# Merging edge keys in groups of four chunks, with a regular order of gathers and adds and no limit registers, in a four-layer graph kernel

## What is computed

```python
h = jnp.maximum(_layernorm(x, axis=-1), 0.0)
agg = jax.ops.segment_sum(edge_attr_32, src, num_segments=3125)
x = x + mlp_with_batchnorm(jnp.concatenate([h, agg], axis=1))
h = jnp.maximum(_layernorm(x, axis=-1), 0.0)
msg = tensor_product(radial(edge_weight), harmonics(edge_attr_3), h[src])
x = x + zeros.at[dst].add(msg)
h = jnp.maximum(_layernorm(x, axis=-1), 0.0)
x = x + three_rounds(h, weighted_adjacency)
h = jnp.maximum(_layernorm(x, axis=-1), 0.0)
x = x + three_rounds_with_batchnorm(h, counted_adjacency)
```

## Time and profile before

| | us |
|---|---|
| median of three runs | 3673.9 |
| the profiled execution | 3668.75 |
| its span in the profile | 3667.0 |
| PE, DVE, ACT, POOL busy | 3008.7, 2849.6, 2416.7, 2168.8 |
| adds on POOL (784), gathers on POOL (784) | 1298.4, 825.8 |

### The profile page before, as it was taken

The page is one execution under the profiler, slowest core; times in us unless marked ns, Lnnn a source line. Parts: engine busy times, 40 slices in busy tenths (PEclk is TensorE's granted clock), DMA queues, the critical chain, the costliest instruction groups (busy, mean ns, idle before and its releaser), DMA issues. The chain is left out here.

```text
span 3667.0 us, 72915 instructions
## 1 busy us (share of the span) xinstructions
PE 3008.7 (82%) x19605; PEld 2412.6 (66%) x19605; DVE 2849.6 (78%) x7391; ACT 2416.7 (66%) x3535; POOL 2168.8 (59%) x1633
## 2 busy tenths in 40 slices
PE   5777688888779999999999999999999946656656
PEld 4667677777667787788788778777777721113246
DVE  6678999998789899899899899899899844341054
ACT  5789799999677777777777777777777712221000
POOL 4037777777468888888888888888888840000000
PEclk9999899999889999999999999999999968788878
DMA  9964333333232333323223223333323239998840
GB/s 391 421 209 62 33 45 46 46 45 44 25 63 47 48 45 48 47 45 48 47 45 49 45 46 48 46 46 47 48 46 47 45 80 427 425 420 352 362 175 5
DMA packets 293446, 422.80 MB, mean 115 GB/s; under 512 B 153015, under 2 KB 228408, under 8 KB 286856
## 3 DMA queue, kind: packets, MB, share of 16 engines
q0 software_dynamic: 149536, 124.64, 20.3%
q1 hardware_dynamic: 127432, 224.50, 18.5%
q10 hardware_dynamic: 16416, 72.92, 4.9%
HBM read 290.44 MB, written 131.45 MB: 115 GB/s over the span
## 5 line engine op out<-in xcount | busy, mean ns | idle before, releaser
L553 POOL DMA_INDIRECT both<-kept x784 | 1298.4, 1656 | 551.8 <-issue 205.4
L881 PEld LDWEIGHTS ps<-prod,big 128*128 128x128 f32 x7840 | 1194.5, 198 | 199.5 <-DVE prod L1211 189.2
L881 PE MATMUL ps<-prod,big 128*128 128x170 f32 x7840 | 1235.9, 319 | 88.8 <-DVE prod L1211 88.8
L562 POOL DMA_INDIRECT kept<-feat_dram,kept x784 | 825.8, 1053 | 288.2 <-issue 204.9
L872 PE MATMUL ps<-prod,onehot 128*128 128x320 f32 x3920 | 693.2, 324 | 155.9 <-DVE prod L1242 155.7
L640 ACT ACTIVATE big<-iota_b,kept 128x640 f32<-128x640 f32 x1078 | 813.0, 814 | 0.0
L872 PEld LDWEIGHTS ps<-prod,onehot 128*128 128x128 f32 x3920 | 594.5, 193 | 171.9 <-DVE prod L1242 164.4
L645 ACT ACTIVATE big<-big 128x2560 f32<-128x2560 f32 x196 | 458.1, 2337 | 360.8 <-PE ps L881 360.7
L938 PE MATMUL ps<-w2mix,kept 65*128 65x384 f32 x1568 | 585.4, 516 | 42.5 <-ACT kept L688 21.7
L1378 DVE TENSOR_REDUCE kept<-kept 128x80 f32<-128x1280 f32 x392 | 562.2, 1475 | 0.0
L938 PEld LDWEIGHTS ps<-w2mix,kept 65*128 65x128 f32 x1568 | 287.8, 195 | 216.1 <-issue 48.4
(11 more groups left out here) (222 smaller groups left out, 3183.0 us busy)
## 6 DMA issues: line engine op xcount, KB each, us to landing
both<-big POOLq DMA_DIRECT2D x40, 2000.0 KB, 99.3
big<-both SPq DMA_DIRECT2D x50, 1600.0 KB, 11.0
kept<-keys_dram SPq DMA_DIRECT2D x392, 128.0 KB
adj_w<-kept ACTq DMA_DIRECT2D x32, 800.0 KB, 32.3
big<-adj_w SPq DMA_DIRECT2D x32, 800.0 KB, 12.4
big<-adj_w ACTq DMA_DIRECT2D x32, 800.0 KB, 11.5
kept<-in_wT SPq DMA_DIRECT2D x196, 128.0 KB
adj_c<-kept ACTq DMA_DIRECT2D x42, 400.0 KB, 31.9
```

Source lines behind the costliest of these rows:

```text
L553: pool.indirect_dma_start(both, bass.IndirectOffsetOnAxis(ap=sc_idx[:, c:c + 1], axis=0), sc_val[:, c // 2, c % 2, :], None, bounds_check= ...
L562: pool.indirect_dma_start(gath[:, s % 2, k, :], None, feat_dram, bass.IndirectOffsetOnAxis(ap=src_i[:, 4 * s + k:4 * s + k + 1], axis=0), ...
L881: mm = pe.matmul(part_sums(part, MSG), onehot[:, q, k, part * P:(part + 1) * P], prod[:, q, k, 0:HI * MSG], start=False, stop=False, skip_ ...
```

## The change

- In the first stage keys are merged in groups of four chunks, one group for two steps: six squares and one 1536-wide rectifier on ACT for a group (`compare_group`), one 512-wide mask (`mark_group`), one set of entries (`group_entries`). The count of live entries passes from chunk to chunk through `merge_open` and three `merge_hop`.
- Keys come in loads of four chunks, edge attributes in loads of 16 chunks (four steps). The high one-hot factor is made once ahead of the stage. `by_act` gives ACT five of 16 one-hots in four steps where it had six; DVE makes eleven where it made ten.
- POOL issues 392 adds ahead of the feature wait instead of 320; then in every second-stage step four gathers and two adds, two steps behind the gathers (`BEHIND`).
- The adds and gathers no longer name a register with the largest allowed index.

```diff
-FIRST = 320
-TAIL = 16
+GROUPS0 = STEPS // 2
 LOADS_AT, SETUP_AT = 13, 16
-BEHIND = 3
+BEHIND = 2
 WSTAGE, CSTAGE = 6, 6
 TO_PROD = 2 * (RING + KEPT - 4)
...
-        near = edge(2, STEPS)
-        keyrow = edge(2, 2 * P)
-        key_gap = edge(6 * P)
-        same = edge(2, 6, P, dt=BF16)
-        same_tri = edge(2, 2, P, dt=BF16)
-        live = edge(2, 2, dt=BF16)
-        high0 = edge(2, 4, HI)
-        offs = sb("offs", [P, 2])
-        attr = sb("attr", [P, 2, 4, FEAT])
+        a_src = rdir[:, :, :].rearrange("p c i -> p (c i)")[:, 0:CH]
+        near = edge(2, GROUPS0)
+        keyrow = edge(2, 4 * P)
+        key_gap = edge(12 * P)
+        same = edge(2, 12, P, dt=BF16)
+        same_tri = edge(2, 4, P, dt=BF16)
+        live = edge(2, 4, dt=BF16)
+        offs = sb("offs", [P, 4])
+        shared = placed[0]
+        high0 = edge(CH, HI)
+        attr = edge(16, FEAT)
+        rows0 = edge(16, 2, FEAT)
+        placed[0] = shared
...
         def by_act(k4):
 
-            return (0, 1) if k4 % 2 else (0,)
+            return (0, 1) if k4 == 3 else (0,)
...
+            def load_group(g, slot):
+
+                if not first(g):
+                    sp.wait_ge(s_gap, 6 * (g - 1))
+                load_keys(4 * g, 4, slot)
+
+            def load_attr(u):
+
+                if not first(u, 1):
+                    sp.wait_ge(s_rows, u)
+                sp.dma_start(attr[:, :, :].rearrange("p k f -> p (k f)"),
+                             ea32_in[:, ds(u * (16 * FEAT), 16 * FEAT)]).then_inc(s_attr, 16)
+
+            def load0(u):
+
+                load_group(u * 2, 0)
+                load_attr(u)
+                load_group(u * 2 + 1, 1)
...
-            last_entry = pool.to_reg(BIG + 4 * P - 1)
-            last_node = pool.to_reg(NP - 1)
-
             def add(c):
 
                 pool.wait_ge(s_idx, c // 2 + 1)
@@ -551,8 +555,7 @@
                 if c >= 2:
                     pool.wait_ge(s_add[c % 2], 16 * (c // 2))
                 pool.indirect_dma_start(both, bass.IndirectOffsetOnAxis(ap=sc_idx[:, c:c + 1], axis=0),
-                                        sc_val[:, c // 2, c % 2, :], None, bounds_check=last_entry,
-                                        compute_op=ALU.add).then_inc(s_add[c % 2], 16)
+                                        sc_val[:, c // 2, c % 2, :], None, compute_op=ALU.add).then_inc(s_add[c % 2], 16)
 
             def gather(s, ks):
 
@@ -560,25 +563,20 @@
                     pool.wait_ge(s_terms, 2 * (s - 1))
                 for k in ks:
                     pool.indirect_dma_start(gath[:, s % 2, k, :], None, feat_dram,
-                                            bass.IndirectOffsetOnAxis(ap=src_i[:, 4 * s + k:4 * s + k + 1], axis=0),
-                                            bounds_check=last_node).then_inc(s_gath[s % 2], 16)
+                                            bass.IndirectOffsetOnAxis(ap=src_i[:, 4 * s + k:4 * s + k + 1], axis=0)
+                                            ).then_inc(s_gath[s % 2], 16)
 
             pool.wait_ge(s_zeroed, 16 * (ZERO_PIECES + 1))
-            for c in range(FIRST):
+            for c in range(CH // 2):
                 add(c)
             pool.wait_ge(s_feat, 16)
             gather(0, range(4))
-            added = FIRST
-            for s in range(STEPS):
-                for half in range(2):
-                    if s + 1 < STEPS:
-                        gather(s + 1, (2 * half, 2 * half + 1))
-                    upto = FIRST + (CH - TAIL - FIRST) * (2 * s + half + 1) // (4 * STEPS) * 2
-                    for c in range(added, min(upto, 2 * (STEPS + s + 1 - BEHIND))):
-                        add(c)
-                        added += 1
-            for c in range(added, CH):
-                add(c)
+            for s in range(STEPS + BEHIND):
+                if s + 1 < STEPS:
+                    gather(s + 1, range(4))
+                if s >= BEHIND:
+                    for c in range(2):
+                        add(2 * (STEPS + s - BEHIND) + c)
...
-            def compare_near(s, q):
-
-                act.wait_ge(s_krow[q], s * 8 - q * 8 + 16)
-                if not first(s, 1):
-                    act.wait_ge(s_same, s)
+            def compare_group(g, slot):
+
+                act.wait_ge(s_krow[slot], g * 8 - slot * 8 + 16)
+                if not first(g, 1):
+                    act.wait_ge(s_same, 2 * g)
+                for lo, n, col, of in ((0, 1, 0, near[:, 0, ds(g, 1)]), (1, 2, 0, key[:, ds(4 * g, 1)]),
+                                       (3, 3, 0, key[:, ds(4 * g + 1, 1)]), (6, 3, 1, key[:, ds(4 * g + 2, 1)]),
+                                       (9, 2, 2, key[:, ds(4 * g + 3, 1)]), (11, 1, 3, near[:, 1, ds(g, 1)])):
+                    act.activation(key_gap[:, lo * P:(lo + n) * P], keyrow[:, slot, col * P:(col + n) * P], ACT.Square,
                                    scale=-1.0, bias=of).then_inc(s_gap, 1)
-                act.wait_ge(s_gap, 4 * s + 4)
-                if not first(s):
-                    act.wait_ge(s_ded, s - 1)
-                act.activation(same[:, q, :, :].rearrange("p b e -> p (b e)"), key_gap[:, :], ACT.Relu, scale=-1.0,
-                               bias=1.0).then_inc(s_same, 1)
+                act.wait_ge(s_gap, 6 * g + 6)
+                if not first(g):
+                    act.wait_ge(s_ded, 2 * (g - 1))
+                act.activation(same[:, slot, :, :].rearrange("p b e -> p (b e)"), key_gap[:, :], ACT.Relu, scale=-1.0,
+                               bias=1.0).then_inc(s_same, 2)
...
+            def merge_hop(g, slot, j):
+
+                pe.wait_ge(s_live, 4 * g + j)
+                mm = pe.matmul(ps[:, 2 + slot, 7 * j:7 * j + 1], same[:, slot, 3 * j - 1, :], live[:, slot, j - 1:j],
+                               start=False, stop=True, skip_group_check=True)
+                if j < 3:
+                    mm.then_inc(s_hop, 1)
+                else:
+                    mm.then_inc(s_ded, 2)
...
             def phase0(s, k4, u):
-                compare_near(s, k4 % 2)
+                if k4 % 2 and not is_last(s):
+                    compare_group(u * 2 + (k4 + 1) // 2, (k4 + 1) // 2 % 2)
                 onehots(0, s, k4 % 2, by_act(k4), dist0, onehot0, b_src)
 
...
+            def mark_group(g, slot):
+
+                dve.wait_ge(s_same, 2 * g + 2)
+                if not first(g):
+                    dve.wait_ge(s_ded, 2 * g - 2)
+                V.tensor_tensor(same_tri[:, slot, :, :], same[:, slot, 1:11:3, :],
+                                earlier[:, :].unsqueeze(1).broadcast_to([P, 4, P]), ALU.mult).then_inc(s_tri, 2)
+
+            def group_entries(g, slot):
+
+                if not first(g, 1):
+                    dve.wait_ge(s_idx, 2 * g)
+                m = ps[:, 2 + slot, 0:28].rearrange("p (j v) -> p j v", j=4)
+                V.tensor_reduce(sc_val[:, ds(2 * g, 2), :, :].rearrange("p d j v -> p (d j) v"),
+                                m[:, :, 1:7].rearrange("p j (v i) -> p j v i", i=3), AX, ALU.add)
+                V.scalar_tensor_tensor(out=offs[:, :], in0=m[:, :, 0], scalar=0.0, in1=to_spare[:, ds(4 * g, 4)],
+                                       op0=ALU.is_gt, op1=ALU.mult).then_inc(s_offs, 2)
+                dve.wait_ge(s_offs, 2 * g + 2)
+                V.tensor_tensor(sc_idx[:, ds(4 * g, 4)], offs[:, :], key[:, ds(4 * g, 4)], ALU.add).then_inc(s_idx, 2)
+
             def mark_earlier(d, q):
...
             def phase0(s, k4, u):
-                q, slot = k4 % 2, k4 // 2
-                mark_earlier(s, q)
-                V.tensor_tensor(high0[:, q, :, :], iota_a[:, :].unsqueeze(1).broadcast_to([P, 4, HI]),
-                                a_src[:, ds(4 * s, 4)].unsqueeze(2).broadcast_to([P, 4, HI]), ALU.is_equal)
-                dve.wait_ge(s_attr[q], 32 * u + 16 * slot + 16)
-                V.tensor_scalar(rows0[:, q, :, 0, :].bitcast(I32), attr[:, q, :, :].bitcast(I32), -4096, None,
-                                ALU.bitwise_and).then_inc(s_hi, 1)
+                q, g, slot = k4 % 2, u * 2 + k4 // 2, k4 // 2
+                if q == 0:
+                    mark_group(g, slot)
                 if not first(s):
                     dve.wait_ge(s_sum[0], 4 * (s - 1))
+                if k4 == 0:
+                    dve.wait_ge(s_attr, 16 * u + 16)
+                    V.tensor_scalar(rows0[:, :, 0, :].bitcast(I32), attr[:, :, :].bitcast(I32), -4096, None,
+                                    ALU.bitwise_and).then_inc(s_hi, 1)
                 for k in range(len(by_act(k4)), 4):
                     ins = V.tensor_scalar(onehot0[:, q, k, :], iota_b[:, :], b_src[:, ds(4 * s + k, 1)], None,
                                           ALU.is_equal)
                 ins.then_inc(s_ohv, 1)
-                dve.wait_ge(s_hi, s + 1)
-                V.tensor_tensor(rows0[:, q, :, 1, :], attr[:, q, :, :], rows0[:, q, :, 0, :],
-                                ALU.subtract).then_inc(s_rows, 1)
```

(25 more changed lines are left out.)

156 lines of the change are left out of this document (71 added, 85 removed).

## The result

The changed kernel takes **3583.2 us** (median of four executions, 3578.6 to 3586.6) against 3673.8 us for the kernel before (four, 3672.5 to 3677.1): ratio 0.9751, 95% interval 0.9734 to 0.9768, 2.5% faster. The forecast was 3573. The profiled execution took 3583.88 us, its span 3582.1.

The account below looks back on a forecast made before the run. POOL was taken to bound the second stage, DVE and ACT the first stage's length. Later gathers +66, second stage -127 and tail -40 took the profiled 3668.75 us to 3567.5; median 5.2 above, 3573 us; range 3535 to 3625.

Parts of the forecast that it names:

- Second stage: Second stage: two adds in every step make steps 9.2 us instead of 9.85; 1816 us against 1943.2, 127 less.
- Rival D: Second stage: PE's clock stays at 0.94 without POOL's waits, 9.67 us a step, 3665 us in all; chance 0.05.
- Tail: Between second stage and rounds: last adds finish before the sums end, so SP loads at once; 40 us less.
- Features: First stage: 4.0 us a step instead of 4.35, feature table at 954 instead of 1023; no gain by itself.
- 392 adds: Ahead of the gathers: 293 adds at 2.29 us, then 99 at 1.87; gathers start at 1089, 66 us later.
- The median: Whole execution: the median lies 5.2 us above the profiled execution, so 3567.5 becomes 3573 us.
- A: Both stages: adds stay at 2.317 us to their end, POOL keeps second-stage steps at 9.3; 3645 us; chance 0.17.
- B: First stage: adds run at 1.87 us from the start, gathers at 966, 3450 us in all; chance 0.12.
- C: First stage: larger loads stretch every add's landing; slower from 2.44 us an add, 3705 us at 2.52; chance 0.11.
- The rule on the shared port: First stage: DVE's one-hots lock POOL out, at most 0.76 us more per add, gathers at 1155, 3639 us.

## Why the prediction was right

The sum, step by step, against the changed kernel's profile:

| | predicted | measured |
|---|---|---|
| feature table | 954 | 946.6 |
| first gather | 1089 | 1114.3 |
| first gather to the end of sums | 1816 | 1806.3 |
| end of sums to SP's load | 0.5 | 0.05 |
| SP's load to the end of the execution | 661.9 (as before) | 663.3 |
| profiled execution | 3567.5 | 3583.9 |

- **Second stage: right.** Even steps ended DVE's waits and PE's clock came back: 9.149 us against 9.2, and the wait in 45 steps is a wait in one. Rival D (the clock stays at 0.94) is out: 0.99. Leaving the registers off was to save 0.3 us of a POOL step; leaving them off saves 0.2 (4 x 0.05), and with them back the step is 9.197.
- **Tail: right**, to half a microsecond.
- **Features: right.** 946.6 for 954, and of no use, as said: the gathers came 168 us later.
- **392 adds: the mechanism held, the size was 25 us short.** Three pieces of it failed. Zeroing ended 10 us later (first add at 243.3 instead of 233.1; with the old merging it is 232.8 to 233.3 in three kernels, and why stays open). The registers were given half of 0.06 us per add in the first stage, 2.29; the add stayed at 2.316. And the adds behind the first stage were to take 1.87 from its end: they took 1.98, since SP's write of the feature table and its first loads of the second stage still cross them (a wait of 3.93 us at 947 and others to 969); from 975 to the end they run at 1.91. The second stage, 10 us quicker than forecast, left 16 of the 25. The median gave 6 of them back by the scatter of executions and by no step of the sum: here it lies 0.7 below the profiled execution, where the one before lay 5.2 above.
- **Rivals.** The first gather, 1114, lies half way between the forecast's 1089 and A's 1141. A missed by its second half: the adds did stay at 2.317 to the end of the first stage, but not behind it, and POOL did not hold the step at 9.3. B is excluded by the cadence. C is excluded in this form: doubled loads of the same size cost 0.12 us an add, and the average over 392 was 2.22, under the 2.44 from which it would have been slower. What the prediction held for it was misread: the adds of 4.06 and 4.88 us do not differ by a load, since SP issues key loads in both (at 849.44 and 854.30).
- **The rule on the shared port.** The prediction let it add every one-hot to the adds, and found a tenth of that. Its 1.62 us is the median of all 784 adds; the 320 of the first stage take 1.69 in the mean, 0.15 over the quickest, which is a fifth of the 0.76. What the runs show is something else: an add is held by a product or a one-hot that has run for more than 0.08 us when the add starts, and only to that operation's end. For the add this agrees with the Trainium skill, page "SBUF — State Buffer", section "SBUF: two separate sides": the shared pair is locked for a whole instruction by whichever came first, and a DVE operation with two SBUF inputs locks it too against a GpSimd operation that reads SBUF. The product has two such inputs. The second stage's reduction has one, and there gathers that start with more than 1 us of it left take 1.00 us; in the kernel before 12 adds that start so take 1.58. For DVE it does not agree: in the changed kernel 17 products start within 0.3 us after an add and take 1.49 us like the others, though the add has 1.2 us or more to go; there the measurement decides.

What the prediction did not see is that the parts stand in for each other: the order is worth 73 us by itself and nothing beside grouping and instructions without limit registers. The 91 us by which the gathers start later are the difference of two terms (1114.3 - 1023.2): 136 for the 72 adds, less 45 that grouping with the old order brings (1023.2 - 978.3).
